# Four small tiles allocated behind all others in a single-core graph layer kernel

## What is computed

```python
u = einsum('bld,bmd->blm', h, h) / sqrt(d)
delta = softmax(u) * adjacency
attn = delta / (sum(delta, axis=2) + 1e-10)
h_left, h_self, h_right = h @ W_left.T + b_left, h @ W_self.T + b_self, h @ W_right.T + b_right
ctx = where(j > i, attn, 0) @ h_left + diag(attn) * h_self + where(j < i, attn, 0) @ h_right
out = layernorm(x + relu(layernorm(ctx) * gamma + beta))
```

## Time and profile before

| | |
|---|---|
| median of the timed runs | 479.48 us |
| the profiled execution | 482.81 us |
| its span, first to last instruction | 481.1 us |
| TensorE busy | 464.3 us, 97% |
| VectorE, ScalarE, GpSimd busy | 360.3, 325.8, 222.2 us |
| mean granted clock of TensorE | 0.985 |

### The profile page before, as it was taken

The page is one execution under the profiler, slowest core; times in us unless marked ns, Lnnn a source line. Parts: engine busy times, 40 slices in busy tenths (PEclk is TensorE's granted clock), DMA queues, the critical chain, the costliest instruction groups (busy, mean ns, idle before and its releaser), DMA issues.

```text
span 481.1 us, 9627 instructions
## 1 busy us (share of the span) xinstructions
PE 464.3 (97%) x2712; PEld 459.5 (96%) x2712; DVE 360.3 (75%) x1088; ACT 325.8 (68%) x715; POOL 222.2 (46%) x294
## 2 busy tenths in 40 slices
PE   8989799999999999999999999999999999999992
PEld 7979799999999999999999999999999999999982
DVE  5667667887777778877777887777788777777756
ACT  6644666677667667766766776676677667667752
POOL 0104543445554444555444455544445554444552
PEclk8999799999999999999999999999999999999998
DMA  8555465465565644556555455655445566544211
GB/s 254 161 162 186 146 187 190 128 194 181 184 188 185 200 138 163 184 176 198 185 172 159 166 183 170 207 185 173 153 165 185 174 207 185 170 156 134 85 71 65
DMA packets 85350, 81.25 MB, mean 169 GB/s; under 512 B 7250, under 2 KB 77396, under 8 KB 85332
## 3 DMA queue, kind: packets, MB, share of 16 engines
q1 hardware_dynamic: 85328, 81.03, 52.6%
q10 hardware_dynamic: 4, 0.00, 0.0%
HBM read 52.17 MB, written 28.84 MB: 168 GB/s over the span
## 4 chain that ended last, share of the span: by engine, by line
PE 88%; DVE 4%; POOL 3%; issue 2%; ACT 2%; SPq 1%; DMA 0%; POOLq 0%; DVEq 0%
PE ps_proj L454 58%; PE ps_ctx L468 19%; PE ps_scores L433 4%; PE ps_scores L442 4%; POOL rstd L976 1%; PE ps_scores L396 1%; SPq L294 1%; POOL shifted L984 1%; ACT normed L576 1%; POOL scaled L980 1%; ACT ps_scores L527 1%; DVE stats L750 1%; DVE y_sb L783 0%; DMA dt_raw<-dt_dram 0%; PE ps_ctx L403 0%
## 5 line engine op out<-in xcount | busy, mean ns | idle before, releaser
L454 PE MATMUL ps_proj<-w_hi,xt_hi 128*128 128x384 f32 x576 | 197.2, 342 | 5.0 <-ACT ps_proj L546 5.0
L454 PE MATMUL ps_proj<-w_lo,xt_hi 128*128 128x384 f32 x576 | 195.9, 340 | 0.0
L454 PE MATMUL ps_proj<-w_hi,xt_lo 128*128 128x384 f32 x576 | 195.8, 340 | 0.0
L976 POOL TENSOR_TENSOR rstd<-var_eps,minus_half 128x4 f32<-128x4 f32 x32 | 42.9, 1340 | 191.7 <-DVE var_eps L769 189.2
L454 PEld LDWEIGHTS ps_proj<-w_hi,xt_hi 128*128 128x128 f32 x576 | 109.6, 190 | 6.5 <-ACT ps_proj L546 6.5
L454 PEld LDWEIGHTS ps_proj<-w_hi,xt_lo 128*128 128x128 f32 x576 | 109.5, 190 | 0.0
L454 PEld LDWEIGHTS ps_proj<-w_lo,xt_hi 128*128 128x128 f32 x576 | 109.3, 190 | 0.0
L550 ACT ACTIVATE proj_hi<-ps_proj 128x384 fp32r<-128x384 f32 x128 | 63.5, 497 | 58.2 <-PE ps_proj L454 58.1
L546 ACT ACTIVATE ps_proj<-bias 128x384 f32<-128x384 f32 (+1 forms) x192 | 92.9, 497 | 0.9 <-DVE proj_lo L735 0.7
L735 DVE TENSOR_TENSOR proj_lo<-ps_proj,proj_hi 128x384 fp32r<-128x384 f32 x128 | 69.7, 548 | 16.9 <-ACT proj_hi L550 14.9
L980 POOL TENSOR_TENSOR scaled<-normed,gamma_sb 128x384 f32<-128x384 f32 x62 | 63.2, 1020 | 36.8 <-ACT normed L576 32.3
(11 more groups left out here) (89 smaller groups left out, 660.4 us busy)
## 6 DMA issues: line engine op xcount, KB each, us to landing
x_sb<-in_x SPq DMA_DIRECT2D x32, 384.0 KB, 4.3
xt_sb<-in_x_t SPq DMA_DIRECT2D x31, 384.0 KB, 3.8
out_dram<-out_sb SPq DMA_DIRECT2D x31, 384.0 KB, 2.9
adj_sb<-in_adj SPq DMA_DIRECT2D x32, 256.0 KB, 4.4
cross_dram<-cross_turned SPq DMA_DIRECT2D x31, 256.0 KB, 2.0
cross_raw<-cross_dram SPq DMA_DIRECT2D x124, 64.0 KB, 2.0
dt_dram<-turned SPq DMA_DIRECT2D x31, 256.0 KB, 2.0
dt_raw<-dt_dram SPq DMA_DIRECT2D x124, 64.0 KB, 2.0
```

Source lines behind the costliest of these rows:

```text
L454: mm = nc.tensor.matmul(ps_proj[bank(at, g)][:, 0:H], stationary, moving[w][:, c, :], start=False, stop=True, skip_group_check=True)
L976: nc.gpsimd.tensor_tensor(rstd[at.slot(2)][:], var_eps[:], minus_half[:], ALU.pow).then_inc(rstd_ready, 1)
```

## The change

The `sb(...)` calls of the four small tiles move from between `bias` and `gamma_sb` to behind `shifted`, the last tile. No instruction is added, taken away or moved, and no wait changes.

```diff
         bias = [sb(f"bias{w}", [P, HE]) for w in range(3)]
-        bias_row = [sb(f"bias_row{w}", [1, H]) for w in (LEFT, RIGHT)]
-        ones_row = sb("ones_row", [1, P])
-        first_read = sb("first_read", [P, 1])
         gamma_sb = sb("gamma_sb", [P, H])
...
         shifted = sb("shifted", [P, T, H])
+
+
+        bias_row = [sb(f"bias_row{w}", [1, H]) for w in (LEFT, RIGHT)]
+        ones_row = sb("ones_row", [1, P])
+        first_read = sb("first_read", [P, 1])
```

## The result

The changed kernel takes 475.38 us (median of 20 runs, 473.36 to 481.44), the kernel before, run beside it, 479.31 us (20 runs, 476.71 to 481.86). The ratio is 0.9914, 95% interval 0.9894 to 0.9934: faster by 0.9%, clear of no change. One of the 20 runs of the changed kernel, that of 481.44 us, counts as slow and is left out of the ratio. The profiled execution took 474.50 us, its span is 472.8 us. The forecast was no change at 479.5 us, with 474.5 to 485.0 for 8 in 10. The time lies within that range, but the forecast of no change was wrong. Rival B had the direction and nearly the size: -4.8 us against a measured -3.9.

The account below looks back on a forecast made before the run. TensorE bounds the steady state through number of matmuls times pace. All terms of the change summed to 0, so the forecast was the median of before, 479.5 us, with 474.5 to 485.0 for 8 in 10.

Parts of the forecast that it names:

- Rival B: Matmuls of L454: operands 32 bytes apart hinder each other less, 2.8 ns off each of 1728; -4.8 us, 474.7 us, chance 0.22.
- What bounds the kernel, and the sum: Steady state on TensorE: time is number of matmuls times pace, 303.4 + 101.4 + 44.0 = 448.8 us of the span.
- The excess over one column a cycle: Matmuls of 384 columns at full clock: 175.6 ns against 160; the 15.6 ns could be operand supply, where an address could count.
- How far the tiles move: Tiles from `gamma_sb` on move down 3616 bytes, 32 past a multiple of 64; only L454's operands move against each other.
- the stationary at remainder 32: Stationary operand starting 32 bytes past a multiple of 64: no steady row showed one; cost taken as 0.
- My own sign for this case: If the stationary's place had its own price, the 45 matmuls' 7.90 us changes 0.078 per 1% of pace, each worth 3.0 us.
- The far end that I named: L454: a gain cannot exceed the 15.6 ns per matmul that are not the array's, 1728 x 15.6 = 27 us.
- The moving operand at 32: Matmuls at L468, L442 and L433: moving operand at remainder 32 or more 64-byte blocks touched costs 0, upper end 1.2 us.
- Rival A: Short 256-column matmuls: weight load touching nine blocks instead of eight becomes their bound, 14.8 ns each; +5.5 us, 485.0 us, chance 0.15.
- Rival C: Transfers before 55 us grow by 1.1 us and bring a lower-clock stretch of 2.9 us; +4.0 us, 483.5 us, chance 0.08.
- The rule of the Trainium skill on where a descriptor starts: Transfers of `turned` and `dt_raw`: starting 224 bytes past a multiple of 256 needs more steps; taken 0, upper end 1.1 us.

Follow-up runs that it names:

- 32 bytes of padding: The kernel before with an unused 32-byte tile behind the bias tiles, the four small tiles left in place; ratio 1.0021, stretch of 27 batches 381.60 us.
- w moved along: The kernel before with an unused 32-byte tile ahead of `w_raw`, so both operands of the projection move by 32; ratio 1.0002, stretch of 27 batches 380.24 us.
- 480 bytes of padding: The kernel before with an unused 480-byte tile behind the bias tiles, the four small tiles left in place; ratio 0.9954, later 0.9912; stretch of 27 batches 376.92 us.
- the map: Layer replaced by stretches of 45 matmuls, each after a short idle time, stationary's start swept 0 to 480 bytes in steps of 32; 173.3 to 176.7 ns for 384 columns.
- the map without idle time between the stretches: Layer replaced by stretches of 45 matmuls with nothing to wait for, operand starts varied; 384 fp32r columns at 173.3 to 177.8 ns, bf16 at 162.5 ns.

## Why the prediction was right or wrong

- *What bounds the kernel, and the sum.* Right. The steady state is the number of matmuls times their pace: 0.123 us a batch turned into 3.9 us of time, nothing was hidden and nothing took its place.
- *The excess over one column a cycle as the place where an address could count.* Right as a place: 15.6 ns before, 13.5 after; with bf16, at the two places tried, 2.5 ns.
- *How far the tiles move, and which line changes its distance.* The count was right: L454 alone. The step from it was wrong. I took the remainder modulo 64 for the whole of the phase. By it L454 and the middle matmuls of L468 stood for distances 0 and 32 and gave equal pace, and I read this as "distance does not matter". Modulo 256 these rows show other pairs, D = 128 for L454, and a different form with paces of its own besides. The trace had rows for neither 160 nor any other distance of 384 columns, so it could not bear the 0 that I put on it.
- *The failed term: the stationary at remainder 32, put at 0.* It measured 2.2 ns on each of the 1728 matmuls of L454, 3.8 us, and it is no price of the stationary's own place: with both operands at remainder 32 the stretch is 380.24 us as before. What has the price is the distance of the moving operand from the stationary modulo 256, which went from 128 to 160. My own sign for this case held: the 45 went from 7.90 to 7.81 us, 1.1%, and at 3.0 us for each 1% that is 3.4 of the 3.9 us. The far end that I named, 15.6 ns, was never near; 173.3 ns, the lowest pace of any stretch of 384 columns, leaves 2.3 ns of the 15.6 to be had.
- *The moving operand at 32, and more blocks touched by* `keys`. Put at 0; attend changed from 175.9 to 175.5 ns within itself, the short ones from 118.8 to 118.1, but the steps to the next group grew. Together they are 8 ns a batch, so 0 was right within 0.3 us in all.
- *Rival A*, the weight load as the bound of the short ones. Wrong: they take 0.72 and 0.71 us where 0.80 was the mark, with the long ones changed instead.
- *Rival B.* Right line, right mark (7.77 forecast for the 45, 7.81 measured), time 0.7 us off. That was luck, for its reason was not right. One of its two rows was misread: of the two matmuls said to stream from remainder 32, one streams from 48. And operands that lie 32 bytes apart are not better as such. With 32 bytes of padding they lie just as far apart modulo 64, and the steady stretch is longer than before, 381.60 against 380.23 us. The changed kernel moved from a bad D of 128 by +32 to a good one of 160; by -32 it would have come to 96, a worse one. The argument that I gave for the sign could not have told the two apart.
- *Rival C*, transfers and clock. Not seen. The wait behind the transfers did not grow: in the changed kernel's profile the two waits are 2.34 and 1.97 us between starts, before they were 2.23 and 3.17. The stretch at the lower clock followed the first (granted clock 0.50 from 35.80 to 37.10 us), while before it had followed the second:

```profile
32.43 0.34 PE L456 MATMUL ps_proj<-w_hi,xt_lo 128*128 128x384 f32 x1
34.77 0.44 PE L456 MATMUL ps_proj<-w_hi,xt_hi 128*128 128x384 f32 x1 [2.00 <-ACT ps_proj L548]
...
50.21 0.34 PE L456 MATMUL ps_proj<-w_hi,xt_lo 128*128 128x384 f32 x1
52.18 0.44 PE L456 MATMUL ps_proj<-w_hi,xt_hi 128*128 128x384 f32 x1 [1.64 <-ACT ps_proj L548]
```

  In both profiles it followed the longer of the two waits, but the length does not decide it. With w moved along it followed a wait of 2.25 us, and in the first profile with 480 bytes of padding a wait of 3.23 us was followed by the upper clock at once (starts 0.17 us apart, granted clock 1.00 from 50 to 62 us):

```profile
50.05 0.34 PE L455 MATMUL ps_proj<-w_hi,xt_lo 128*128 128x384 f32 x1
53.27 0.44 PE L455 MATMUL ps_proj<-w_hi,xt_hi 128*128 128x384 f32 x1 [2.89 <-ACT ps_proj L547]
...
53.73 0.34 PE L455 MATMUL ps_proj<-w_hi,xt_lo 128*128 128x384 f32 x1
53.90 0.34 PE L455 MATMUL ps_proj<-w_hi,xt_hi 128*128 128x384 f32 x1
```

- *The rule of the Trainium skill on where a descriptor starts* ("DMA: Bandwidth & Descriptors", "How a descriptor splits into AXI transactions") was weighed against a row of 1.93 us. The traces agree with it in direction, and show how little it is worth here. Of the 13 profiled runs that compute the layer, that of the kernel before is the only one with `turned`, `dt_raw`, `cross_turned` and `cross_raw` at multiples of 256 bytes, and its median times from issue to landing are the shortest for all four: 2.04, 2.00, 2.01 and 1.96 us, against 2.06, 2.02, 2.05 and 1.99 in the changed kernel (medians of the single issues in the traces; the pages round the stores to 2.0 and 2.1, the loads to 2.0). That is 0.02 to 0.05 us, not the 0.26 and 0.84 us of my upper end. No run isolates the start as the cause.
- *The Trainium skill on the load of the stationary* ("TensorE: Matmul & The Clock Gate", "LDWEIGHTS (loading the stationary operand)"): its 107 ns for 128 columns had spoken against rival A, and rival A fell. A stretch of 256 columns without `keys` at D=192, with another stationary block for each matmul, goes at 113.3 ns, so a load takes no more than that, and the page's figure agrees.

## What to carry to other kernels

When TensorE bounds a kernel with 4-byte operands, the place of the operands in memory is a parameter worth a few runs: pad between the tiles of the stationary and those of the moving operand in steps of 32 bytes through one period of 256, and read the pace of matmuls from starts over a long steady stretch, where it repeats to 0.01 us when the time of the run scatters by several. Don't compute the best padding from a map of one form and one distance: the projection followed such a map as long as all its distances were equal, with two alternating ones it went at 174.6 ns where the map had 173.3, and attend did not follow it at all. And an edit that only moves tiles, or that adds a small tile ahead of large ones, can change the time by 1% with no instruction changed; before crediting a gain to an edit, look whether it shifted the operands.

## What the runs showed of the hardware that I had not expected

- At a granted clock of 1.00, matmuls of 384 fp32r columns went at 173.3 ns at best and 177.8 at worst by the places of their operands; bf16 at 162.5 ns at both places tried, neither of them a slow one for fp32r. At the lower clock they take 320 ns, one column a cycle.
- The distance between stationary and moving operand counts with a period of 256 bytes, for 384 columns and starts at multiples of 32 bytes. Good, 173.3 ns: 0, 64, 160, 192, 224 (192 took 174.6 once, entered without idle time); bad: 96 with 176.7 and 128 with 176.0; 32 has two stable paces, 173.3 and 176.7 ns, in one and the same execution.
- Starts that are not multiples of 32 bytes can cost too: 177.8 ns at m=24, 177.8 at 40, 175.6 at 16, but 173.3 at 8; with both starts at 16, so D = 0, 175.7 (all in the map without idle time between the stretches, so that states may have been inherited).
- The paces come as fixed cycles of starts, such as 175, 182, 176, 173, 174 ns, that repeat in every batch or every second one, with transfers and three other engines running beside them. Which cycle a stretch falls into can depend on what ran before: one and the same stretch of 386 columns went at 173.3 ns after idle time and at 177.8 straight after 384-column matmuls. A short idle time does not make stretches begin alike.
- Open: what in the memory or in TensorE makes the period of 256 bytes and the floor 13.3 ns above one column a cycle, and why the number of stationary columns changes the pace out of step with its size.
